# The x product of twelve tiles is computed while W_dec streams in, and the x loads move behind x_free

## What is computed

```
U = (mu @ W_dec + b_dec).reshape(B, 513, 30);  param = U @ V
x = x + x @ param[:, :-1] + param[:, -1]
h = ln(ln(x) * pw_g[path] + pw_b[path]) * cp_g[comp] + cp_b[comp]
t = ln(x) * tm_g[comp] + tm_b[comp];   s = ln(x) * ms_g[scale] + ms_b[scale]
m, n, r = x + MLP_LN(memory), x + MLP_LN(noise), x + MLP_LN(resource)
cat = [w0*h, w1*t, w2*m, w3*n, w4*r, w5*s]
out = x + ln(silu(cat @ int_W1 + b1) @ int_W2 + b2) * g + be
```

## Time and profile before

| | |
|---|---|
| median of 3 runs | 664.78 us |
| the profiled execution | 664.47 us, span 662.7 us |
| TensorE busy | 616.4 us, 93% |
| VectorE, GpSimd, ScalarE busy | 454.7, 398.3, 130.3 us |
| moved by DMA | 98.55 MB |
| from 200 to 600 us | TensorE busy all the time |

### The profile page before, as it was taken

How to read it: one execution, slowest core, us unless ns; L and a number is a source line. 1 busy time by engine, 2 the same in 40 slices (tenths; PEclk the granted TensorE clock), 3 DMA queues, 4 the chain that set the end, 5 groups by cost and what they waited for, 6 DMA issues and landing times.

```text
span 662.7 us, 9289 instructions
## 1 busy us (share of the span) xinstructions
PE 616.4 (93%) x2878; PEld 465.9 (70%) x2878; DVE 454.7 (69%) x817; ACT 130.3 (20%) x212; POOL 398.3 (60%) x439
## 2 busy tenths in 40 slices
PE   4877887799999999999999999999999999999991
PEld 0111445688888888888888888888888888888871
DVE  0220498877777777777777777777777777777732
ACT  2011442122222221122222221111222222222110
POOL 1021587766666667766677776666666766666410
PEclk9675998799999999999999999999999999999996
DMA  8999966344444434443444344444343334443000
GB/s 290 385 376 378 335 196 180 116 131 132 129 127 121 134 110 134 121 128 128 126 125 133 125 129 120 127 117 130 125 129 125 132 119 132 123 128 89 16 33 16
DMA packets 52175, 98.55 MB, mean 149 GB/s; under 512 B 10937, under 2 KB 23738, under 8 KB 52027
## 3 DMA queue, kind: packets, MB, share of 16 engines
q1 hardware_dynamic: 37856, 55.38, 24.9%
q0 software_dynamic: 12160, 42.04, 21.4%
q10 hardware_dynamic: 2144, 0.96, 0.5%
HBM read 89.85 MB, written 8.39 MB: 148 GB/s over the span
## 4 chain that ended last, share of the span: by engine, by line
PE 85%; DMA 6%; DVE 4%; POOL 3%; issue 1%; SPq 0%; ACT 0%; POOLq 0%; DVEq 0%
PE bank L562 22%; PE bank L563 22%; PE bank L564 22%; PE bank L556 8%; DMA stage<-in_W_dec 3%; DMA raw<-in_W_dec 3%; PE bank L586 2%; PE bank L536 2%; PE bank L518 2%; PE bank L598 1%; PE bank L600 1%; PE bank L608 1%; PE bank L489 1%; POOL xop L711 0%; DVE W L852 0%
## 5 line engine op out<-in xcount | busy, mean ns | idle before, releaser
L562 PE MATMUL bank<-W,ops 128*128 128x512 f32 x384 | 155.2, 404 | 1.8 <-DVE W L828 1.6
L563 PE MATMUL bank<-W,ops 128*128 128x512 f32 x384 | 152.4, 397 | 0.0
L564 PE MATMUL bank<-W,ops 128*128 128x512 f32 x384 | 152.0, 396 | 0.0
L668 POOL TENSOR_SCALAR ve<-mv 128x1 f32<-128x1 f32 x96 | 26.4, 275 | 104.3 <-DVE mv L882 101.7
L562 PEld LDWEIGHTS bank<-W,ops 128*128 128x128 f32 x384 | 72.5, 189 | 18.5 <-DVE W L828 1.8
L564 PEld LDWEIGHTS bank<-W,ops 128*128 128x128 f32 x384 | 72.5, 189 | 17.6
L563 PEld LDWEIGHTS bank<-W,ops 128*128 128x128 f32 x384 | 72.6, 189 | 16.1
L449 ACT ACTIVATE ops<-bank 128x512 fp32r<-128x512 f32 x96 | 54.0, 599 | 85.1 <-PE bank L556 85.1
L705 POOL TENSOR_TENSOR h<-xhat,pwt 128x512 f32<-128x512 f32 x32 | 57.2, 1786 | 21.5 <-DVE xhat L960 21.5
L672 POOL TENSOR_TENSOR rs<-ve,mhalf 128x1 f32<-128x1 f32 x96 | 64.9, 677 | 8.0
L473 ACT ACTIVATE z<-bank 128x512 f32<-128x512 f32 x32 | 19.2, 600 | 248.4 <-PE bank L564 248.4
(11 more groups left out here) (122 smaller groups left out, 1004.9 us busy)
## 6 DMA issues: line engine op xcount, KB each, us to landing
stage<-in_W_dec SPq DMA_DIRECT2D x11, 960.0 KB, 12.5
xT<-in_xT SPq DMA_DIRECT2D x32, 256.0 KB
x<-in_x SPq DMA_DIRECT2D x32, 256.0 KB, 5.9
out<-y SPq DMA_DIRECT2D x32, 256.0 KB
raw<-in_int_W SPq DMA_DIRECT2D x6, 1024.0 KB, 13.9
raw<-in_W_dec SPq DMA_DIRECT2D x5, 960.0 KB, 14.2
idxrep<-in_rows SPq DMA_DIRECT2D x64, 32.0 KB, 4.4
stage<-in_mlp_W SPq DMA_DIRECT2D x1, 1024.0 KB, 5.5
```

The lines of the kernel that those rows point to most:

```text
L562: nc.tensor.matmul(bank[:, :], op[:, HI, c, :], w[:, HI, c, :], start=start and c == 0, stop=False)
L563: nc.tensor.matmul(bank[:, :], op[:, HI, c, :], w[:, LO, c, :], start=False, stop=False)
L564: last = nc.tensor.matmul(bank[:, :], op[:, LO, c, :], w[:, HI, c, :], start=False, stop=stop and c == KC - 1)
```

## The change

- M, N, R of int_W1 are loaded first (12 loads of 256 KB), and WX is summed and split in quarters by ScalarE and VectorE.
- Between the decodes, TensorE runs `prefill(p)`: the x product of tile p+2, p from 0 to 11, whose transposed rows come into `stash`; ScalarE copies the result back into the same place. In steps 2 to 13 (`kept`) TensorE skips the x product, and VectorE adds the stash to the sum ahead of silu.
- The MLPs come behind the decodes. The second layer, V.W and the offsets run with one chunk of K on each of four groups of 32 columns, are copied to `part` by ScalarE and summed by a selection matmul. Their VectorE work stands in `first_step`.
- To make room, `xT` loses its buffer: `xraw` is the low half of `xop`. Its load waits for `x_free`.
- Constants come in one load, u is replaced by o, the loop starts at step 15 instead of 3.

```diff
-FIRST, LAST = 3, TILES - 3
+PRE0, NPRE = 2, 12
+PRE_AFTER = (1, 2, 3, 5, 6, 7, 9, 10, 11, 13, 14)
+FIRST, LAST = PRE0 + NPRE + 1, TILES - 3
...
+def kept(t):
+    return t.i is None and PRE0 <= t.s < PRE0 + NPRE
...
+        xraw = [sb_at(at_xop + (2 * s + LO) * ROW, f"xraw{s}", [P, KC, P]) for s in range(2)]
...
+            def load_x(a):
+                s, old = a.slot, a.plus(-2)
+                if old.exists():
+                    sp.wait_ge(x_free, old.count())
+                sp.dma_start(xraw[s][:, :, :], d["xT"][s, bass.ds(a.pair(), 1), :, :, :].rearrange(
+                    "o p c t -> (o p) c t")).then_inc(xT_in[s], 16)
...
+            for j in range(2 * DECS):
+                decode(j)
...
+                if j in PRE_AFTER:
+                    prefill(PRE_AFTER.index(j))
+            for p in range(len(PRE_AFTER), NPRE):
+                prefill(p)
...
+            def prefill(p):
+                if p == 0:
+                    pe.wait_ge(wx_lo, KC)
+                if p >= 2:
+                    pe.wait_ge(pre_stash, p - 1)
+                pe.wait_ge(pre_lo, p + 1)
+                product(HID[p % 2], pre_op(p), W1[:, X, :, :, :], True, True).then_inc(pre_used, 1)
...
+            def low_rank(m):
+                if kept(m):
+                    pe.wait_ge(z_ready, m.count(extra=-1))
+                return nc.tensor.matmul(HID[m.slot][:, :], stack[:, m.slot, :], VWst[:, :], start=kept(m), stop=False)
...
+            def mlp_second(m):
+                wait_ring(pe, MLP2[m])
+                for c in range(KC):
+                    last = nc.tensor.matmul(pPART[c * Q:(c + 1) * Q, :], LM[:, m, c, :], staged(MLP2[m])[:, c, :],
+                                            start=(m == 0), stop=(m == 2))
+                last.then_inc(mlp_used, 1)
+
+            def sum_parts(sel, got, done):
+                pe.wait_ge(got, 1)
+                nc.tensor.matmul(pSUM[0:sel.shape[-1], :], sel, part[:, :], start=True, stop=True).then_inc(done, 1)
...
                 if m.exists():
-                    if m.plus(-2).exists():
+                    if not (kept(m) or second):
                         pe.wait_ge(z_ready, m.count(extra=-1))
-                    product(HID[m.slot], xop[:, m.slot, :, :, :], W1[:, X, :, :, :], True, False)
+                        product(HID[m.slot], xop[:, m.slot, :, :, :], W1[:, X, :, :, :], True, False)
+                    last = low_rank(m)
+                    if not second:
+                        last.then_inc(x_free, 1)
+                    offsets(m)
...
+                if c.exists() and kept(c):
+                    v.wait_ge(hid_ready, c.count())
+                    v.wait_ge(zT, c.count(extra=0))
+                    nc.vector.tensor_tensor(z[:, :], HID[c.slot][:, :], stash[:, c.s - PRE0, :],
+                                            ALU.add).then_inc(z_whole, 1)
```

More of the change, by code:

```diff
@@ L81, in is_first, with steps @@
     return t.i is None and t.s == 0
-def steps(eng, emit):
-    for n in range(-2, FIRST):
+def kept(t):
+    return t.i is None and PRE0 <= t.s < PRE0 + NPRE
+def steps(eng, emit, first):
+    for n in range(first, FIRST):
         emit(Tile(n))
@@ L442, in split_w2, with x_high @@
[L442 to L444 removed]
+            def x_high(a):
+                s = a.slot
+                act.wait_ge(xT_in[s], a.slot_count(16))
+                nc.scalar.activation(xop[:, s, HI, :, :], xraw[s][:, :, :], ACT.Copy).then_inc(x_hi, 1)
+            pre_high(0)
+            pre_high(1)
+            for j in range(2 * DECS):
+                if j % 2 == 1:
+                    evacuate(j // 2)
+                if j in PRE_AFTER:
+                    p = PRE_AFTER.index(j)
+                    if p + 2 < NPRE:
+                        pre_high(p + 2)
+                    pre_keep(p)
+                if j == 2 * DECS - 2:
+                    x_high(Tile(0))
@@ new lines, in _, with x_product @@
+            for p in range(len(PRE_AFTER), NPRE):
+                prefill(p)
+            wait_ring(pe, MLP1)
+            for c in range(4):
+                last = nc.tensor.matmul(pM[0:C, :], cond[:, c, 0:C], staged(MLP1)[:, c, :],
+                                        start=(c == 0), stop=(c == 3))
+            last.then_inc(mlp_used, 1)
+            def x_product(m):
+                pe.wait_ge(x_lo, m.count())
+                pe.wait_ge(pre_stash, NPRE - 1 + m.s)
+                product(HID[m.slot], xop[:, m.slot, :, :, :], W1[:, X, :, :, :], True, False).then_inc(x_free, 1)
@@ new lines, in embed @@
+            def embed(f):
+                pe.wait_ge(x_lo, f.count())
+                if is_first(f):
+                    pe.wait_ge(ust_ready, 1)
+                if f.plus(-1).exists():
+                    pe.wait_ge(stack_ready, f.count(extra=0))
+                for q in range(KC):
+                    last = nc.tensor.matmul(XU[:, 0:2 * P], Ust[:, f.batch, q, :], xop[:, f.slot, :, q, :],
+                                            start=(q == 0), stop=(q == KC - 1))
+                last.then_inc(xu_ready, 1)
@@ L812, in _, with one_hot @@
-            last.then_inc(lm_ready, 1)
+                                           op0=ALU.add, op1=ALU.add).then_inc(ub_ready, 1)
+            for p in range(2, NPRE):
+                pre_low(p)
+            def one_hot(a):
+                s = a.slot
+                v.wait_ge(rep_in[s], a.slot_count(32))
+                if a.plus(-2).exists():
+                    v.wait_ge(x_used, a.count(extra=-1))
+                nc.vector.tensor_scalar(OH[:, s, :], idxrep[:, s, :], inquad, None, ALU.is_equal).then_inc(oh_ready, 1)
```

1066 lines of the change are left out of this document (580 added, 486 removed).

## The result

The changed kernel takes **756.74 us** (median of 4 runs, 750.21 to 759.46) against 665.18 us: a ratio of 1.136, 95% interval 1.128 to 1.144. It is slower by 92 us. The profiled execution took 755.89 us for a span of 754.1, 91.4 us over the span of before (662.7).

A forecast was written before the change was run, and what follows sets the result against it. TensorE, busy 93%, was taken to bound the kernel except at the start. From 664.5 us, 28 steps lengthened from 16.9 to 20.6 us, less 3, add 101 and the start 0: 765 us, range 724 to 815.

The forecast's parts named there:

- kept steps: Steps 2 to 13: VectorE's stretch from rstd to x_free, 11.1 us, keeps each near 20.6 us, hiding the x product's saving.
- the start: Time up to step 2: earlier x products and later MLPs give nothing on balance, 0, from -12 to +12 us.
- the loop: Steps 14 to 29: about 20.6 us each, where TensorE's own work is 16.9.
- the end: Steps 30 and 31, claimed to stay as they are.
- The ring: x_free, idx, gathers, rstd, xhat, split of h, H product, next step's x_free: a closed chain of 20.6 us per step.
- The 3.5 us that I took for idx: Landing of idx behind its issue on SP, taken as the shortest landing of the idxrep reads.
- rival 1: Quiet queue: idx and idxrep land in about 2.0 us each, period 19.1 us, 724 us; chance 0.2.
- Rival 3: x_free does not decide: loop stays at 16.9 us, kept steps about 16.0, 654 us; chance 0.04.
- VectorE's lag: In kept steps, VectorE's add of the stash stands behind y of the step before; the first kept step, without it, 3 us less.
- the sign of this: Kept steps 2.8 us shorter than the loop's would show the claim about VectorE's lag wrong.
- The wait ahead of the product with W2: TensorE waits about 2 us in a step, through x_high ahead of the split of z; hidden by the ring, 0.
- Rival 2: Landings stay at their medians, or TensorE's gaps bring its clock to 1.2 GHz; 819 us by the medians; chance 0.15.

The follow-up runs named there:

- Run 1: Kernel before with one wait changed: the load of xT for tile n+2 waits for x_used of tile n instead of x_lo; 788.29 us, ratio 1.183.
- run 4: Changed kernel with 10 parked tiles instead of 12 and two xT buffers of its own, the load waiting for x_lo; 668.10 us.
- run 8: Changed kernel with x, idx and idxrep ahead of xT on SP and x_high behind the splits of z and h; 667.45 us, ratio 1.003.
- Run 7: Changed kernel with ScalarE's x_high behind the splits of z and h and VectorE's one_hot behind the split of z; 758.17 us.
- Run 5: Changed kernel with low_rank in kept steps waiting for z of tile n-1 instead of tile n-2; 779.57 us.
- Run 9: run 4 with the low halves of T, S, H and W2 all on VectorE, W2's behind the offsets; 664.71 us, ratio 0.999.
- the ten-tile runs: Changed kernel with 10 parked tiles instead of 12, without and with two xT buffers of its own; 759.57 us and 668.10 us.
- Run 6: Changed kernel with ScalarE's x_high moved behind the splits of z and h from step 1 on; 757.81 us.
- run 2: Changed kernel with x, idx and idxrep loaded ahead of xT on SP; four executions of 793.6, 792.7, 792.5 and 712.0 us.

## Why the prediction was right and wrong

The time came out 8 us under the forecast of 765. That closeness is in good part luck. Behind it are misses of opposite sign: kept steps 31 us too dear, the start 16 too cheap, the loop 5, the end 2.

- **The ring: right, but not alone.** Foreseen 20.6 us per loop step, measured 20.15 in a step at full clock and 20.91 on average. Run 1 shows that the wait alone makes it, run 4 that it goes when the buffer is not shared, run 8 that it goes when idx and idxrep are not behind the wait and x_high is not ahead of the splits. Run 7, in the steps at full clock, has the ring over the split of h by itself at 20.1 to 20.4. What the prediction missed is that the path over idxrep, one_hot, x1, the split of z and the products with W2, S and H closes a ring as long: it had the product with W2 start 5.7 us behind x_free, and it starts 6.7 us behind low_rank's end (577.54 to 584.20). The loop's share, 16 x 3.7 = 59 us by the sum, was 64. The 3.5 us that I took for idx from its issue to the gathers was 3.3, by two errors that cancel. The profile's list of issues has idx landed sooner, at a median of 2.5 us:

```profile
idx<-in_idx SPq DMA_DIRECT2D x32, 1.5 KB, 2.5
```

  In the step at 573.04 the chain that ended last has 2.5 us for this landing and 0.7 us from it to the first gather, a hand-over for which the sum had less than 0.1. So rival 1's landing of 2.0 us was nearer than mine, with two transfers of 256 KB in front of idx. The Trainium skill, "DMA: Bandwidth & Descriptors", section "Anatomy of one DMA — SWDGE (gpsimd) path", has about 2 us as the fixed cost of a transfer on GpSimd's path; idx, on SP's, was about 0.5 us above that. Rival 3 is excluded in the loop, but its 16.0 us for a kept step outside the ring is what runs 4 and 8 measure (15.8).
- **The kept steps: wrong, by 2.9 us each.** The failed step is "The ring hardly shortens, because another stretch takes over ... 11.1 us from rstd to x_free". I let low_rank of tile n+1 wait for z of tile n. `z_ready` with `count(extra=-1)` is the count of the tile two back, which has long been written. TensorE in a kept step of the changed kernel

```profile
311.61 0.60 PE L577 MATMUL bank<-cst,tt 128*128 128x128 f32 x4
...
312.95 0.40 PE L644 MATMUL bank<-VWst,stack 128*128 128x512 f32 x1
```

  and ScalarE's silu of the tile before beside it:

```profile
314.83 0.63 ACT L553 ACTIVATE z<-z 128x512 f32<-128x512 f32 x1 [11.40 <-DVE z L1156]
```

  low_rank starts at 312.95 without a wait, 2.5 us before that z is ready. A kept step at full clock takes 17.0 to 17.3 us, and five in which the clock falls take 18.4 to 18.9; the average is 17.75. The ring less the x product, 20.0 - 2.8 = 17.2, agrees with the first figure, but that it is the ring that sets it is not shown: TensorE waits for the split of h in only three kept steps, for 0.2 to 0.3 us. VectorE's lag is still there, by another way. In every kept step TensorE waits 0.9 to 2.4 us for the stack, which stands on VectorE behind y and the new add. In the same step:

```profile
316.01 0.49 PE L639 MATMUL bank<-Vst,stack 128*128 128x512 f32 x1 [2.43 <-DVE stack L1017]
```

  In steps 5 to 7 the chain that ended last goes through that lag (xhat, GpSimd's h, o, y, the add) once in two steps, and the two take 34.5 us (210.03 to 244.50), 17.2 each. Run 5 puts the wait where I had read it and gets 20.1. The text had named the sign of this: kept steps 2.8 us shorter than the loop's (they are 3.2 shorter). Priced right, this term is 12 x 0.8 = 10 us; mine was 12 x 3.7 - 3 = 41.
- **The start: wrong, by 15.7 us**, outside the 12 that I allowed. Ust is ready at 82.4 (79 foreseen), from there to step 1 are 46.6 us (38), step 1 takes 24.3 (20). I had costed each of VectorE's operations at its duration in a quiet stretch and GpSimd's halves of the blocks as lying beside them. They don't. VectorE, at the first stack and at the gains of h of tiles 0 and 1, the second just ahead of step 1:

```profile
84.78 3.41 DVE L1015 CAST stack<-inner 128x128 fp32r<-128x128 f32 x1
...
106.09 3.23 DVE L1064 TENSOR_TENSOR ht<-ht,ctt 128x512 f32<-128x512 f32 x1
...
126.34 4.92 DVE L1064 TENSOR_TENSOR ht<-ht,ctt 128x512 f32<-128x512 f32 x1
```

  and GpSimd at those times:

```profile
84.52 2.36 POOL L844 TENSOR_TENSOR W<-ring,W 128x1024 fp32r<-128x1024 f32 x1
86.84 1.26 POOL L819 TENSOR_TENSOR xop<-xraw,xop 128x512 fp32r<-128x512 f32 x1
...
105.68 0.78 POOL L858 TENSOR_TENSOR vrs<-vrs 6x1 f32<-6x1 f32 x1 [2.52 <-DVE vrs L1083]
106.44 2.33 POOL L844 TENSOR_TENSOR W<-ring,W 128x1024 fp32r<-128x1024 f32 x1
...
125.98 4.72 POOL L868 TENSOR_TENSOR W<-ring,W 128x2048 fp32r<-128x2048 f32 x1
```

  TensorE waited 5.3, 5.6 and 3.8 us behind them (stack, ht, BT), and after the last it ran at half clock for a while (0.50 granted from 135 to 141). Run 9 removes the overlap and gets back 3.4 us of the 15.7. The other 12 were not taken apart; that the ten-tile runs start at most 0.4 us earlier speaks against the parked products, and what is left is one chain through VectorE on which MLPs, V.W and offsets now stand in line with tiles 0 and 1.
- **The wait ahead of the product with W2: costed at 0, wrong.** I had foreseen TensorE's wait there (some 2 us; 2.0 to 2.9 measured), put it down to ScalarE's x_high and called it hidden. Run 6 shows that one_hot on VectorE makes it as well. It is hidden by a few tenths at most, and it is one piece of idle time behind which the clock can fall: 20.0 becomes 21.3 in such steps. Rival 2 named the clock; it came in part, in the loop some 0.8 us a step.
- **The aim of the change**: even with the ring removed (run 8) a parked tile saves 16.9 - 15.8 = 1.1 us of its 2.8, since in a kept step TensorE waits for VectorE's stack (0.9 us idle) and split of t (0.3), with the start of a product after each. Twelve tiles are 13 us, against 15.7 us of longer start. That is why run 8 stands at 667.5 and not below 665.

## What to carry over

When two uses come to share a buffer, follow what its refill waits for through the in-order queue that issues it: here a load of 256 KB waited by design, but idx, 1.5 KB, and idxrep, 64 KB, were queued behind it, and x_high, which needs the load itself, stood ahead of the splits on ScalarE. Changing these orders alone (run 8) took 89 us off. Take waits by their counts, not by their names; one tile more or less decides whether a chain is in a ring. Where a step has two waits, price the second by itself, since the path behind it can be as long as the first. And where a loop has slack left, look for what stands behind a landing on every other engine before calling a wait hidden, because idle time of TensorE in one piece can be paid for a second time in clock.

## What the runs showed of the hardware

- Some operations of VectorE are held until GpSimd's are over. The stack's copy (0.23 us alone) ended at 88.19, just behind GpSimd's two operations in a row (86.88 and 88.10); both gains of h (0.69 alone) ended 0.55 us behind GpSimd's (109.32 and 108.77, 131.26 and 130.70). In the loop's steps st takes 1.78 us where tt of the same form takes 0.69, beside GpSimd's h. Not all are held: in the step at 573.04 tt starts 0.05 us ahead of GpSimd's h (587.22 and 587.27) and takes 0.69, and the sum into inner, which reads a PSUM bank, takes 0.29 us at 576.01 beside GpSimd's xb (575.79 to 577.10), the same as at 97.90 with GpSimd idle. Run 9 is the counter-test: without GpSimd's halves the three held operations take 0.23, 0.69 and 0.69. The Trainium skill, "SBUF — State Buffer", section "SBUF: two separate sides", describes an exclusive lock on a pair of ports that the two share; the ends agree. By that page whichever starts first has the lock, and the starts agree too: the gain at 106.09 starts ahead of the operation at 106.44, but behind GpSimd's vrs, which runs from 105.68 to 106.46.
- The clock makes a ring's slack uncertain. In the changed kernel's loop, gaps of 2.0 to 2.9 us ahead of the product with W2 were followed by matmuls at half clock in eight steps, and gaps of the same length were not in the other eight. In run 2, where the gaps were 3.2 to 4.7 us, the half clock followed in all sixteen; that program took 712 us in one execution and 793 in three.
- The same read of 256 KB, xT, landed 2.6 us behind its issue in run 1 (median) and was there for ScalarE only 6.2 and 5.9 us behind it in the steps shown of runs 2 and 8, beside store and gathers.
